# Weight splits with four buffers, a gate product in two halves, and three groups of work in another place

## The reference

```python
mixed = hidden_states @ w_qkv                # q, k: 16 heads of 128; v: 32 heads of 128
z = (hidden_states @ w_z).reshape(B, S, HV, DV)
y = conv over 4 taps of mixed;  mixed = silu(y)
q, k = l2norm(q) * DK ** -0.5, l2norm(k)
def step(Sm, inp):                            # 512 steps
    Sm = Sm * exp(g); kv = k . Sm; delta = (v - kv) * beta
    Sm = Sm + k (x) delta; o = q . Sm
on = og * rsqrt(mean(og * og) + EPS) * norm_w     # og = o * silu(z)
return on @ w_out
```

## Time and profile before

| | |
|---|---|
| median of three runs | 3352.64 us |
| the profiled execution | 3348.56 us, its span 3346.8 us |
| PE busy | 3070.1 us (92%), 28176 instructions |
| DVE busy | 2658.9 us (79%) |
| ACT busy | 1863.1 us (56%) |
| POOL busy | 561.1 us (17%) |
| granted TensorE clock over the span | 0.967 |

### The profile page before, as it was taken

The page is one execution under the profiler, slowest core; times in us unless marked ns, Lnnn a source line. Parts: engine busy times, 40 slices in busy tenths (PEclk is TensorE's granted clock), DMA queues, the critical chain, the costliest instruction groups (busy, mean ns, idle before and its releaser), DMA issues. The chain is left out here.

```text
span 3346.8 us, 75945 instructions
## 1 busy us (share of the span) xinstructions
PE 3070.1 (92%) x28176; PEld 2379.8 (71%) x28176; DVE 2658.9 (79%) x6397; ACT 1863.1 (56%) x6019; POOL 561.1 (17%) x861
## 2 busy tenths in 40 slices
PE   2799999999999999999999999999999999748999
PEld 0677777777777777777777777777777777526665
DVE  5588887878787878787878888888878887679984
ACT  3465666666565556566655665656666565433332
POOL 0120111111121211121211121211111111053320
PEclk7799999999999999999999999999999999858999
DMA  5433323233333233332333232333232333020000
GB/s 210 133 92 90 98 87 102 68 95 93 99 90 98 86 95 90 99 93 79 87 90 100 89 98 88 95 89 98 87 103 69 94 91 90 11 92 19 23 13 19
DMA packets 398179, 288.22 MB, mean 86 GB/s; under 512 B 230098, under 2 KB 361298, under 8 KB 379860
## 3 DMA queue, kind: packets, MB, share of 16 engines
q1 hardware_dynamic: 397812, 283.36, 28.3%
HBM read 232.58 MB, written 50.73 MB: 85 GB/s over the span
## 5 line engine op out<-in xcount | busy, mean ns | idle before, releaser
L944 DVE SCALAR_TENSOR_TENSOR conv<-xb,convw,conv 128x512 f32<-128x512 f32 x768 | 570.9, 750 | 113.8 <-ACT conv L666 95.6
L479 PE MATMUL bank<-wout,onT 128*128 128x512 f32 x1024 | 509.7, 621 | 22.0 <-issue 22.0
L491 PE MATMUL bank<-x_hi,w_hi 128*128 128x512 f32 x1024 | 431.0, 421 | 17.5 <-POOL w_lo L1010 16.2
L491 PE MATMUL bank<-x_hi,w_lo 128*128 128x512 f32 x1024 | 401.5, 392 | 0.0
L491 PE MATMUL bank<-x_lo,w_hi 128*128 128x512 f32 x1024 | 399.9, 391 | 0.0
L662 ACT ACTIVATE xb<-bank 128x512 f32<-128x512 f32 x256 | 164.2, 642 | 364.4 <-PE bank L491 364.4
L500 PE MATMUL bank<-w_hi,x_hi 128*128 128x256 f32 x1024 | 295.9, 289 | 0.0
L479 PEld LDWEIGHTS bank<-wout,onT 128*128 128x128 f32 x1024 | 175.1, 190 | 165.0 <-issue 153.9
L500 PE MATMUL bank<-w_lo,x_hi 128*128 128x256 f32 x1024 | 289.5, 283 | 0.0
L500 PE MATMUL bank<-w_hi,x_lo 128*128 128x256 f32 x1024 | 289.1, 282 | 0.0
L1005 POOL COPY halo<-xb 128x12 f32<-128x12 f32 x256 | 68.3, 267 | 1117.7 <-ACT xb L662 1117.7
(11 more groups left out here) (231 smaller groups left out, 7211.7 us busy)
## 6 DMA issues: line engine op xcount, KB each, us to landing
x_hi<-x_hi_scratch SPq DMA_DIRECT2D x64, 1024.0 KB, 5.0
x_lo<-x_lo_scratch SPq DMA_DIRECT2D x64, 1024.0 KB, 8.2
decay<-decay_scratch SPq DMA_DIRECT2D x64, 512.0 KB, 5.6
M_scratch<-M SPq DMA_DIRECT2D x128, 256.0 KB, 2.3
w_raw<-in_w_proj SPq DMA_DIRECT2D x64, 384.0 KB, 4.0
Tc<-T_scratch SPq DMA_DIRECT2D x64, 128.0 KB, 2.4
wout<-in_w_out SPq DMA_DIRECT2D x16, 512.0 KB, 3.2
xT<-in_x_chunks SPq DMA_DIRECT2D x1, 4096.0 KB, 12.5
```

Source lines behind the costliest of these rows:

```text
L479: mm = pe.matmul(banks[4 + b][:], lhsT=onT[:, j, b, :], rhs=t["wout"][:, j, :], start=j == 0, stop=j == 1)
L491: mm = pe.matmul(banks[j % 2][:].rearrange("p (b t) -> p b t", b=B), lhsT=t[f"w_{p}"][:, k, j, :], rhs=t[f"x_{q}"][:, k], start=i == 0, st ...
L944: dve.scalar_tensor_tensor(out=y3, in0=xb[:, :, i:i + C], scalar=t["convw"][:, j, i:i + 1], in1=y3, op0=ALU.mult, op1=ALU.add).then_inc(on ...
```

## The change

1. `w_raw` gets four buffers; the room comes from `junk`, which goes. SP issues a head's four weight fetches in one go at the start of the iteration, ahead of `x_hi` and `x_lo` of it; ACT waits for all four and rounds them one behind the other after `gate(r + 2, 1)`, ahead of `join_a`; before, the four stood at three places of its loop.
2. The squares are written over their own input in PSUM, and ACT waits for its own copy `K` before them.
3. Where r % 4 = 0, `project(r + 2, 0)` of PE stands ahead of `gram(r + 1)`.
4. `gate(r + 2, 3)` of PE is cut into its first and last six products, and `turn(r)` stands behind the first six, ahead of `y_part(r + 1, 0)`; the last six follow that.
5. DVE runs one tap of projection 1 (all three where r % 4 = 0) ahead of `factors(r)`.

```diff
-                                 ("w_raw", 2, 6, 128), ...
+                                 ("w_raw", KT, 6, 128), ...
-        def fetch_w(h, k):
-            if 4 * h + k >= 2:
-                sp.wait_ge(on["w_lo"], 4 * h + k - 1)
-            sp.dma_start(t["w_raw"][:, k % 2], a["w_proj"][h, :, k]).then_inc(on[f"d_w{k % 2}"], 16)
+        def fetch_w(h):
+            if h:
+                sp.wait_ge(on["w_lo"], KT * h)
+            for k in range(KT):
+                sp.dma_start(t["w_raw"][:, k], a["w_proj"][h, :, k]).then_inc(on["d_w"], 16)
...
-        def gate(s, b):
+        def gate(s, b, terms=range(len(TERMS))):
...
+            if ahead and r % NC == 0:
+                project(r + 2, 0)
             if solve:
                 gram(r + 1)
-            if ahead:
+            if ahead and r % NC:
                 project(r + 2, 0)
...
             if ahead:
-                gate(r + 2, 3)
+                gate(r + 2, 3, range(0, 6))
+            if state:
+                turn(r)
             if solve:
                 y_part(r + 1, 0)
-            if state:
-                turn(r)
+            if ahead:
+                gate(r + 2, 3, range(6, 12))
...
+                    act.wait_ge(on["K_read"], s + 1)
                 for b in range(B):
-                    n = 4 * k + b
-                    op = act.activation(t["junk"][:, n], bank[:, b * C:(b + 1) * C], ACT.Square, accum_out=t["sums"][:, n:n + 1])
+                    n, row = 4 * k + b, bank[:, b * C:(b + 1) * C]
+                    op = act.activation(row, row, ACT.Square, accum_out=t["sums"][:, n:n + 1])
...
-                act.wait_ge(on[f"d_w{k % 2}"], 16 * (2 * (s // NC) + k // 2 + 1))
+                act.wait_ge(on["d_w"], 16 * KT * (s // NC + 1))
...
             if fresh:
-                split(r + 3, 0)
+                for k in range(KT):
+                    split(r + 3, k)
             if solve:
                 join_a(r + 1)
             if ahead:
                 silu(r + 2, 3)
-            if fresh:
-                split(r + 3, 1)
             if solve:
                 join_b(r + 1)
-            if fresh:
-                split(r + 3, 2)
-                split(r + 3, 3)
...
             if state:
                 output(r)
                 update(r)
+            early = TAPS - 1 if r % NC == 0 else 1
+            if ahead:
+                taps(r + 2, 1, range(early))
+            if state:
                 factors(r)
             if ahead:
-                taps(r + 2, 1)
+                taps(r + 2, 1, range(early, TAPS - 1))
                 taps(r + 2, 2)
```

More of the change, by code:

```diff
@@ L35 @@
 SETUP_SEMS = "d_first d_in d_scratch x_split ones zeroed ab yrow exs w_plus ln gates cums others ends betas tokens tok_copied".split()
-ATTENTION_SEMS = """d_x d_w0 d_w1 d_conv d_decay d_ends d_wout d_M d_N d_T d_Tc
+ATTENTION_SEMS = """d_x d_w d_conv d_decay d_ends d_wout d_M d_N d_T d_Tc
     w_hi w_lo proj halo xb y save tap silu z z_read
@@ L90, in decoder_kernel @@
                                  ("xb", 4, B, C + TAPS - 1), ("conv", 4, B * C), ("halo", 4, B, TAPS - 1),
-                                 ("w_raw", 2, 6, 128), ("decay", HJ, B, C), ("E", HJ, B, C),
-                                 ("M", B, HJ, C), ("P0", B, HJ, C), ("P1", B, HJ, C), ("sums", 8), ("junk", 8, C), ("small0", 72),
+                                 ("w_raw", KT, 6, 128), ("decay", HJ, B, C), ("E", HJ, B, C),
+                                 ("M", B, HJ, C), ("P0", B, HJ, C), ("P1", B, HJ, C), ("sums", 8), ("small0", 72),
                                  ("small1", 72), ("K0", B, DH), ("K1", B, DH), ("Vn0", B, HJ, DH), ("Vn1", B, HJ, DH),
@@ L289, in sync @@
             if n < NS and n % NC == 0:
-                fetch_w(n // NC, 0)
-                fetch_w(n // NC, 1)
+                fetch_w(n // NC)
             if 0 <= p < NS and p % NC == 0:
@@ L324, in sync @@
                     sp.dma_start(t[f"x_{part}"][:].rearrange("p k b t -> p (k b t)").bitcast(F32), scratch[f"x_{part}"][n % NC]).then_inc(on["d_x"], 16)
-            if n < NS and n % NC == 0:
-                fetch_w(n // NC, 2)
-                fetch_w(n // NC, 3)
     def tensor(pe):
@@ L498, in gate @@
                 pe.wait_ge(on["y"], 4 * s + 3 + half)
-            for n, (k, p, q) in enumerate(TERMS):
+            for n in terms:
+                k, p, q = TERMS[n]
                 mm = pe.matmul(banks[half][:, i * 256:(i + 1) * 256], lhsT=t[f"x_{p}"][:, k, b, :], rhs=t[f"w_{q}"][:, k, 4:6, :],
                                start=n == 0, stop=n == len(TERMS) - 1)
-            if i == 1:
+            if i == 1 and n == len(TERMS) - 1:
                 mm.then_inc(on["z"], 1)
@@ L693, in split @@
                     act.wait_ge(on["z"], 2 * s)
-                act.wait_ge(on[f"d_w{k % 2}"], 16 * (2 * (s // NC) + k // 2 + 1))
-                act.activation(t["w_hi"][:, k], t["w_raw"][:, k % 2], ACT.Copy).then_inc(on["w_hi"], 1)
+                act.wait_ge(on["d_w"], 16 * KT * (s // NC + 1))
+                act.activation(t["w_hi"][:, k], t["w_raw"][:, k], ACT.Copy).then_inc(on["w_hi"], 1)
         for r in range(-3, NS):
@@ L934, in out, with taps @@
             dve.tensor_tensor(t["acc"][:, b, s % NC, :], banks[4 + b][:], t["acc"][:, b, s % NC, :], ALU.add).then_inc(on["acc"], 1)
-        def taps(s, j):
+        def taps(s, j, which=range(TAPS - 1)):
             xb, y3 = t["xb"][:, j], t["conv"][:, j].rearrange("p (b t) -> p b t", b=B)
-            for i in range(TAPS - 1):
+            for i in which:
                 n = 12 * s + 3 * j + i
@@ L1009, in split @@
                 pool.wait_ge(on["w_hi"], 4 * (s // NC) + k + 1)
-                pool.tensor_tensor(t["w_lo"][:, k], t["w_raw"][:, k % 2], t["w_hi"][:, k], ALU.subtract).then_inc(on["w_lo"], 1)
+                pool.tensor_tensor(t["w_lo"][:, k], t["w_raw"][:, k], t["w_hi"][:, k], ALU.subtract).then_inc(on["w_lo"], 1)
         for r in range(-3, NS):
```

## The result

| kernel | runs | median us | range | profiled execution | its span |
|---|---|---|---|---|---|
| before | 12 | 3352.55 | 3344.11 to 3356.37 | 3348.56 | 3346.8 |
| changed | 12 | 3359.2 | 3353.46 to 3364.29 | 3364.29 | 3362.4 |

The ratio is 1.0021, with a 95% interval of 1.0012 to 1.003: 6.7 us slower, 4 to 10. A second set of ten runs gave 1.0027 (1.0017 to 1.0036). The forecast was 3376 (3326 to 3397): the sign is right, the size is not.

What follows compares the result with a forecast made beforehand. PE, 92% busy, was taken to bound the kernel through its waits; 30 - 8 + 0 - 1 + 2 = +23 us on 3352.64 gave 3376 us, range 3326 to 3397.

Steps and rivals of the forecast that it cites:

- the sign: Whole kernel slower, +23 us; said to hang on whether DVE's six copies have to wait for POOL.
- What bounds: PE is 92% busy, so only its idle time or work counts; POOL and DVE shut each other out.
- The splits, +2.0 us a head, +30: Behind weight splits, w_lo and DVE's copies take turns, delaying join_b and read: 2.0 us more for each of 15 heads.
- Projection 0, -8: At gram where r % 4 = 0, 1.7 us of waiting goes, partly returning for P: half a microsecond, 16 times.
- Half gate and turn, 0: In 62 iterations, waits at the Y part and out are exchanged for one for R: 0, between -36 and +18 us.
- My bound for it, +0.3 us an iteration: Upper bound for half gate and turn: an extra tile-size switch and a factor chain delayed by the moved tap.
- Squares in PSUM, 0 with a bound of +20: ACT's squares before gram: 0 taken; 20 us in all if each of eight squares cost 0.15 us more.
- The start, -1: The 16.2 us wait for w_lo at the start shrinks by 1 us, between 3 off and 2 on.
- r = 62, +2: In r = 62, which has no gate, the Y part stands behind a turn that waits for R: +2 us.

Runs made afterwards that it cites:

- the turn alone: The kernel before with the last gate product in halves, the output turned ahead of the Y part, and the taps moved for it: 3368.0 us, ratio 1.0044.
- `w_lo` held: The changed kernel with two waits on POOL: second w_lo behind DVE's last join copies, third behind E's scans: 3314.9 us, ratio 0.9895.
- the held pair: The changed kernel with those two waits on POOL, 3314.9 us, against the kernel differing from it only by gate halves and early turn, 3268.5 us.
- the first experiment: The kernel before with four weight buffers, the four splits together and squares in PSUM, without PE's new order: 3374.9 us, ratio 1.0073.
- acc later: The kernel before with one DVE memset of 512 columns ahead of out(2) in iterations r % 4 = 1: 3354.4 us, ratio 1.0017.

## Why the forecast was wrong

- **What bounds.** Right: PE's idle places, and POOL and DVE that shut each other out. A DVE copy from SBUF to SBUF beside `w_lo` waits until the other's instruction is over, four of the six in each head of the changed kernel. The Trainium skill (SBUF — State Buffer, Who interferes with whom) says that the one that comes second blocks fully while the other holds the shared pair for its instruction. The trace agrees: the four waited 1.1 to 1.6 us, beside `w_lo` of 1.81 each.
- **The splits, +2.0 us a head, +30: the step that failed.** I let both engines pay in turns, so that POOL's 7.2 us became 8.1, and had `read` wait for acc again behind it. POOL paid nothing (7.25 us for four), join_b waited 1.75 us (and join_a 0.6) instead of some 3.4, and `read` not at all, as no `w_lo` stands beside the scans any longer. The kernel with the rest of the change takes 91.2 us for the two iterations of such a head without the new splits, and 91.3 and 91.2 with them. On top of the rest the 15 heads cost 1 us (3359.2 against 3358.2, less than the runs can tell), not 30.
- **The clock: a term that was missing.** I had read the waits by their length alone. Eight stretches of low clock take 1.7 us each from PE, but delay the next head's gram by only 0.5, so they are about 4 of the 11.7 us by which the loop is longer. That the medians differ by 7 to 10 us and the first profiled pair by 15.7 is in part that this execution was the slowest of its twelve; why, stays open.
- **Projection 0, -8.** Right in place, low in size: -12 (7 to 16). I had put all of gram's 27.0 us into 16 iterations, where only 19.7 stand (1.2 us each, not 1.7), but `P` takes 0.3 us back and not 0.7.
- **Half gate and turn, 0: wrong as well.** The whole term, with its taps, costs 16 us by itself. The exchange of two waits (0.35 and 0.34 us) for one for `R` of about the same size came out (0.67 us in each iteration of the turn alone), but I called the moved tap worth nothing "but where DVE itself is late". DVE was late, at every Y part: the row of 0.24 us that I had cited said so. The tap alone is worth -26 us, and the turn costs more than that: 36 us in the whole change, 46 with `w_lo` held, and 42 from the tap alone (-26) to halves, turn and taps (+16), each against its own runs of before. My bound for it, +0.3 us an iteration, counted one more switch between tile sizes; measured in the held pair are 0.26 us of busy time and 0.5 of idle time.
- **Why the sign came out.** By luck. Without the turn the kernel is 27 us faster than before, and the turn takes 36 back: what is left is +7 to +10. The forecast had its plus from the splits, which add 1 on top of the rest.
- **Squares in PSUM, 0 with a bound of +20.** Alone they cost 13 us. In the changed kernel PE does not wait for them (2.1 us once): where r % 4 = 0 projection 0 stands ahead of gram, and behind the new splits gram's wait is gone, as in the first experiment. So the 0 held because of the change's other parts. The Trainium skill (ScalarE: Activation LUTs, Step-by-step: what each stage is for) says that PSUM is the quicker destination for ScalarE. One square does take 262 ns instead of 300, but eight of them ended 3.67 us into the iteration and not 3.30: they start 0.2 us later behind the copy of `K`, and stand further apart.
- **The start, -1, and r = 62, +2.** The wait at the start is 16.3 us, so 0. In r = 62 the wait for `R` grew from 2.5 to 4.5 us while that of 1.0 for `Xc` went: of the size that I took.

## What to carry to other kernels

Price each instruction that an edit moves as if it were the whole edit: here one moved tap was worth 26 us and the reordering it was moved for cost 36 to 46, while the forecast had 0 for both. A run of each part alone would have kept the tap.

A wait of the engine that bounds the kernel can have a second price, what the clock does behind it. Ask the granted clock of short windows behind every wait of more than a microsecond, before and after; the page's tenths of 40 slices show none of this. But do not take half of a low stretch as its cost. Where a stretch stands in some of equal places, lay the places side by side and see when the next group starts: here PE lost 1.7 us and the next head only 0.5, because a wait for another engine was shorter by the rest.

## What the runs showed of the hardware

- TensorE's clock falls from 2.4 to 1.2 GHz for 3.4 us (6.8 in five cases) behind waits of 1.75 us at join_b and 2.3 to 2.4 us at join_b or in `read`, in five to ten of 15 equal places. Behind the wait of 1.83 us in `read` it fell in none of 30 (both profiles of before), so the wait's length alone does not decide it. (One stretch stands elsewhere, at 39 us of r = 50 with the squares alone; why, is open.) Which of equal places are hit changes from one execution to the next.
- A stretch of 3.4 us delays PE's next groups by 0.5 us in the changed kernel and by 1.4 us with acc later; one of 6.8 us in the first experiment by 2.1.
- Where POOL's `w_lo` and DVE's copies shut each other out, `w_lo` was not delayed at all (7.25 us for four, 1.80 for one alone), while four of six copies waited 1.1 to 1.6 us each. The loss was DVE's alone. With `w_lo` beside wide scans before, POOL paid as well: 4.55 us for two.
- Squares of ACT with their own PSUM row as destination: 262 ns each against 300 to SBUF, and a group of eight that ends 0.37 us later.
